# Two layer norms ahead of a state-space stage, moved from VectorE to ScalarE and GpSimd, with the norm's affine folded into the projections

## The chip, the cores and the metric

One Trainium2 chip, one core. The metric is the device time of the kernel in microseconds (us); lower is better. TensorE (PE), VectorE (DVE), ScalarE (ACT), GpSimd (POOL) and SyncE (SP, which here only issues transfers) each run an instruction stream of their own, in order, and wait for each other on semaphores. "In order" is the thing to keep in mind: an instruction whose operands are ready still waits for everything ahead of it on its engine.

## The reference, cut to what matters

Two blocks follow each other on x of shape (4, 2048, 256), fp32. Only the head of the first block matters here:

```python
h  = layernorm(x) * (1 + ca) + sa                       # first norm, modulated by row vectors
mu = mean(h); var = mean((h - mu) ** 2)
xn = (h - mu) / sqrt(var + 1e-5) * norm_w + norm_b      # second norm, of the state-space stage
z    = xn @ W_in
gate = silu(xn @ W_gate)
dt   = clip(softplus(z @ W_dt + b_dt), 0.001, 1.0)
Bp, Cp = z @ W_B, z @ W_C
# 16 states, scanned over time:  state = exp(dt * A) * state + (dt * Bp * z);  y_t = sum_s state_s * Cp_s
y = scan(...) * gate
x = x + ga * (h + y @ W_out)
# then: a second norm and a gelu FFN (block 0); attention-like scan, RWKV and two expert FFNs (block 1)
```

## The kernel before, in words

**Tiles.** The 8192 tokens are cut into 16 chunks of 512. Channels by tokens or tokens by channels, a chunk is 128 partitions wide. Weights and the activations that feed them are split into a high and a low part, and such a product is three matmuls (`split3`, line 1548).

**Streams.** Every engine's order is written out ahead by `weave`. The backbone is the state-space stage of chunk i: 23 empty marks, 68 units (16 states by 4 blocks of 128 channels, and 4 more to drain), then a tail that gates y, turns it, multiplies by W_out and adds. Three side streams are merged into the backbone by the table `PACE`, which gives each piece of a stream the backbone step ahead of which it is issued: `n_stream` (the front of the stage: both norms, xn, the projections, dt), `f_stream` (block 0's FFN, one chunk behind) and `x_stream` (block 1, two chunks behind). A step number below zero lies in the steps of the chunk before. One engine's pieces of one stream keep their order.

**A unit.** For unit u (state s, channel block d) ACT computes exp(dt * A) into one of two PSUM banks (A0, A1; line 1105), POOL computes its input z * B into one of four buffers `bu` (line 960), DVE runs the scan (line 1329), PE turns the result to tokens (four transposes, line 1543) into bank H0 or H1, and DVE adds it, times C, into `acc` (the read-out, line 1279). ACT may fill a bank once the scan two units back has read it; POOL may fill a buffer once the scan four units back is done.

**The norms ahead of the stage.** On DVE, for the four token tiles of a chunk: `stats` (bn_stats line 1251, bn_aggr line 1255), POOL takes the power -0.5 (line 947), DVE centres and scales (lines 1263, 1268, with the modulation rows `cA0`, `sA0`), `stats` again, POOL's power and bias (lines 951, 953), and ACT applies it (`n_norm`, line 1040). PE turns n; ACT evicts it with norm_w as scale and norm_b as bias into `xnf` (line 1052) and copies the high part `xnh` (line 1057); DVE subtracts for `xnl` (line 1301). `bu` lies over `xnh` and `xnl`, and the projections use banks A0 and A1, so they can't start before the last scan of the chunk before. In the table the DVE pieces `mean0`, `norm0`, `mean1` stand at -4, -4, -3: behind the last unit, ahead of the tail's `out`.

**The tail.** DVE multiplies `acc` by the gate in token layout (`gated`, line 1339), PE turns it (`y`), ACT copies it out (line 1118), PE multiplies by W_out (line 1564), DVE adds.

**PE's order from the last units on**: h2T of block 1 between units 63 and 64, the four last turns of the scan, the four kq products, y, kvT, btT, out0, qsT, out1, then xn0, xn1, ao0, ao1, then bc, dt, gate, ct, z (the front's 78 matmuls of 512 columns and a few small ones), then block 1's xlT and the FFN's c0 to c7.

Of the kernel before, what the change touches and what calls it, by code (L numbers as in the profile page):

```python
# [145 lines left out]
def since(eng, sig, chunk, k=0):  # L146

    if sig.at(chunk, k) > 0:
# [10 lines left out]
    },  # L159
    "pool": {  # L160
        "rstd0": -157, "rstd1": -108, "gx": 3, "u0": 20, "u1": 21, "u2": 27, "u3": 27, "xg": 95, "rstd_a": 103,
        "x_prob": 147, "rstd_e": 187, "x_bias": 190, "rstd_h": 209, "rstd_i": 210, "rstd_j": 214, "rstd_m": 241,
        "x5": 286,
    },
    "act": {
# [1646 lines left out]
```

## Time and profile before

| | |
|---|---|
| median of 3 runs | 3481.04 us (3476.44 to 3485.96) |
| the profiled execution's own time | 3472.46 us |
| its span, first to last instruction | 3470.7 us |
| busy, share of the span: PE | 2944.9 us (85%) |
| DVE | 2869.9 us (83%) |
| ACT | 2037.2 us (59%) |
| POOL | 1748.8 us (50%) |
| mean granted TensorE clock | 0.925 |
| first scans of chunks 5, 6 and 7 start at | 1066.3, 1261.2, 1457.5 us |
| last scans of chunks 5, 6 and 7 end at | 1202.6, 1398.0, 1596.8 us |

So a chunk takes some 196 us: some 137 us from its first scan to its last, and some 59 us from there to the first scan of the next. The shares say that PE and DVE are close to each other and that neither is full; they do not say where which of them is waited for. In the rows below a timeline row is: start, duration, engine, line, operation, tiles out<-in, count, and in brackets how long the engine sat idle ahead of it and who ended that. A group row is: line, engine, operation, tiles, shapes, count, then busy us in total, mean ns of one, and idle us ahead of it.

### The profile page before, as it was taken

To read this page: it belongs to the slowest core of one execution; us is meant where nothing else is said; L and a number is where in the kernel's file an instruction comes from. 1 tells how busy PE (TensorE), PEld (TensorE's weight loads), DVE (VectorE), ACT (ScalarE), POOL (GpSimd) and SP (SyncE) were. 2 spreads that over 40 slices of the span, in tenths; PEclk is the share of its full clock that TensorE was granted. 3 is DMA by queue.
4 is the path that set the end of the run, shared out by engine and by line. 5 is a ranking of instruction groups with operands and counts; after the bars stand their busy time and mean duration, and the time that the engine had idled before them with its cause. 6 is when DMAs were issued, how large, how long until landed. Compare 5 with 4: busy or idle time off the path is not lost. (4 is left out here: it accounts for less than half of the span.)

```text
span 3470.7 us, 45595 instructions
## 1 busy us (share of the span) xinstructions
PE 2944.9 (85%) x15032; PEld 2409.8 (69%) x15032; DVE 2869.9 (83%) x5084; ACT 2037.2 (59%) x3393; POOL 1748.8 (50%) x1389
## 2 busy tenths in 40 slices
PE   3567599898989899898989989898989899897957
PEld 1446478687777778687777778677777778676746
DVE  4596979898998989798998979899898979798231
ACT  0436476665757576665757576665757566574423
POOL 0555556464755656464755646464655646464010
PEclk7659599999999999999999999999999999998979
DMA  7112122231323223231312323131312323031302
GB/s 242 45 46 61 37 95 101 81 108 54 124 68 113 84 95 101 78 110 56 122 64 103 101 95 101 63 117 63 117 65 93 114 92 104 32 126 56 110 30 79
DMA packets 152906, 307.66 MB, mean 89 GB/s; under 512 B 18376, under 2 KB 97116, under 8 KB 135260
## 3 DMA queue, kind: packets, MB, share of 16 engines
q1 hardware_dynamic: 152128, 301.60, 26.1%
q8 instruction: 121, 1.98, 0.2%
q10 hardware_dynamic: 272, 1.57, 0.1%
q0 software_dynamic: 272, 1.57, 0.1%
q14 instruction: 113, 0.93, 0.1%
HBM read 287.35 MB, written 17.36 MB: 88 GB/s over the span
## 5 line engine op out<-in xcount | busy, mean ns | idle before, releaser
L960 POOL TENSOR_TENSOR bu<-z,bb 128x512 f32<-128x512 f32 x1024 | 1299.9, 1288 | 494.6 <-DVE hs L1329 303.7
L1105 ACT ACTIVATE ps_A<-dt,a_neg 128x512 f32<-128x512 f32 x1024 | 701.5, 687 | 606.6 <-DVE hs L1329 603.3
L1329 DVE TENSOR_TENSOR_SCAN hs<-ps_A,state,bu 128x512 f32<-128x512 f32 x768 | 974.4, 1273 | 37.1 <-ACT ps_A L1105 19.4
L1543 PE MATMUL ps_H<-ident,hs 128*128 128x128 f32 x4096 | 652.0, 298 | 222.4 <-DVE acc L1279 125.4
L1543 PEld LDWEIGHTS ps_H<-ident,hs 128*128 128x128 f32 x4096 | 520.7, 152 | 360.0 <-DVE acc L1279 164.1
L1662 PE MATMUL ps_B<-ws_out,hid 128*128 128x256 f32 x3072 | 722.1, 381 | 18.2 <-ACT hid L1243 10.5
L1279 DVE SCALAR_TENSOR_TENSOR acc<-ps_H,ctok,acc 128x512 f32<-128x512 f32 x960 | 697.5, 728 | 21.9 <-PE ps_H L1543 19.0
L1662 PEld LDWEIGHTS ps_B<-ws_out,hid 128*128 128x128 f32 x3072 | 568.7, 190 | 101.7 <-ACT hid L1243 15.5
L1548 PE MATMUL ps_B<-fh,ws_in 128*128 128x512 f32 x1536 | 572.1, 418 | 8.3 <-ACT cb L1215 4.2
L1548 PEld LDWEIGHTS ps_B<-fh,ws_in 128*128 128x128 f32 x1536 | 290.0, 189 | 69.0 <-ACT cb L1215 10.4
L1329 DVE TENSOR_TENSOR_SCAN hs<-ps_A,bu 128x512 f32<-128x512 f32 x256 | 309.7, 1211 | 27.0 <-ACT ps_A L1105 19.5
L1548 PE MATMUL ps_B<-fl,ws_in 128*128 128x512 f32 x768 | 301.0, 392 | 0.0
L1241 ACT ACTIVATE hid<-ps_B 128x512 f32<-128x512 f32 x256 | 150.7, 589 | 151.2 <-PE ps_B L1548 150.8
L1548 PE MATMUL ps_B<-f1h,ws_in 128*128 128x512 f32 x512 | 189.4, 433 | 53.9 <-DVE lg L1361 24.2
L990 POOL TENSOR_TENSOR z<-z,dt 128x512 f32<-128x512 f32 x64 | 88.4, 1382 | 164.3 <-ACT dt L1090 164.3
L1548 PEld LDWEIGHTS ps_B<-f1h,ws_in 128*128 128x128 f32 x512 | 104.8, 205 | 90.0 <-DVE lg L1361 25.7
L1243 ACT ACTIVATE hid<-hid 128x512 f32<-128x512 f32 x256 | 161.7, 632 | 8.2
L1548 PEld LDWEIGHTS ps_B<-fl,ws_in 128*128 128x128 f32 x768 | 146.1, 190 | 20.5
L1519 DVE SCALAR_TENSOR_TENSOR hA<-ps_B,coef,hA 128x256 f32<-128x256 f32 x192 | 79.6, 476 | 94.9 <-PE ps_B L1662 93.3
L1396 DVE TENSOR_TENSOR fl<-ff,fh 128x512 fp32r<-128x512 f32 x64 | 47.6, 784 | 132.2 <-ACT fh L1177 132.2
L951 POOL TENSOR_TENSOR rs_x<-rs_x,mhalf 128x4 f32<-128x4 f32 x48 | 52.9, 1103 | 190.1 <-DVE rs_x L1259 190.1
L947 POOL TENSOR_TENSOR rs_s<-rs_s,mhalf 128x4 f32<-128x4 f32 x16 | 18.9, 1184 | 206.3 <-DVE rs_s L1259 206.3
(245 smaller groups left out, 4566.0 us busy)
## 6 DMA issues: line engine op xcount, KB each, us to landing
ws_in<-w_split SPq DMA_DIRECT2D x128, 1024.0 KB, 5.0
bb<-b_rows SPq DMA_DIRECT2D x256, 256.0 KB, 4.0
ws_out<-in_L_ffn_V_rwkv SPq DMA_DIRECT2D x64, 512.0 KB, 5.6
ws_out<-in_L_ffn_W SPq DMA_DIRECT2D x32, 512.0 KB, 5.8
w_split<-ws_in SPq DMA_DIRECT2D x8, 1024.0 KB, 5.2
xb<-in_L_attn_x SPq DMA_DIRECT2D x16, 512.0 KB, 7.3
n<-in_L_attn_x SPq DMA_DIRECT2D x16, 512.0 KB, 3.9
out<-xb SPq DMA_DIRECT2D x16, 512.0 KB, 2.8
```

The costliest lines, as they stand in the source:

```text
L951: pool.tensor_tensor(rs[:, :], rs[:, :], mhalf[:, :], ALU.pow).then_inc(own_sig.sem, 1)
L960: pool.tensor_tensor(bu[:, u % 4, :], z[:, d, :], bb[:, s % 2, :], ALU.mult)\
L990: pool.tensor_tensor(z[:, k, :], z[:, k, :], dt[:, k, :], ALU.mult).then_inc(s_u.sem, 1)
L1105: act.activation(b.t[:, :], dt[:, d, :], ACT.Exp, scale=a_neg[:, d, s:s + 1])\
L1241: act.activation(hid[:, k, :], b.t[:, :], ACT.Relu).then_inc(b.free, 1)
L1243: act.activation(hid[:, k, :], hid[:, k, :], ACT.Square).then_inc(x_sq.sem, 1)
L1279: dve.scalar_tensor_tensor(out=acc[:, t, :], in0=b.t[:, :], scalar=ctok[:, t, s:s + 1], in1=acc[:, t, :], op0=ALU.mult, op1=ALU.add).then_ ...
L1329: dve.tensor_tensor_scan(hs[:, s % 2, d, :], b.t[:, :], bu[:, k % 4, :], state[:, s, d:d + 1] if i % CPB else 0.0, ALU.mult, ALU.add)\
L1519: ins = dve.scalar_tensor_tensor(out=hA[:, t, :], in0=b.t[:, t % 2 * C:(t % 2 + 1) * C], scalar=coef[:, t, e:e + 1], in1=hA[:, t, :], op0= ...
L1543: return pe.transpose(dst, src, ident[:, :])
L1548: last = pe.matmul(dst, a, b, start=n == 0, stop=n == len(prods) - 1)
L1662: last = pe.matmul(b.t[:, t % 2 * C:(t % 2 + 1) * C], hid[:, k, t * P:(t + 1) * P], wt[:, k % HB, :], start=k == 0 and t % 2 == 0, stop=k ...
```

## The change

- DVE's pieces `mean0`, `norm0`, `mean1` and the two powers of `n_stream` on POOL are replaced. ACT sums a token tile with an activation that has an accumulator output (`sum0`), POOL makes the negative mean, ACT sums the squares of x minus mean (`sq0`, Square with bias), POOL makes rstd and the bias (`rstd0`), ACT normalizes in place (`norm0`), POOL multiplies by `cA0` and adds `sA0` (`h0`: two operations on 128x1024), and the same for the second norm (`sum1`, `sq1`, `norm1`).
- norm_w is multiplied into the high and low parts of W_in, W_gate, the product W_in W_dt and the narrow weights; norm_b goes through the weights into bias columns (`in_col`, `bdt_col`). This is done once, in the setup. ACT's eviction into `xnf` goes; `xnh` and `xnl` are made from PSUM.
- The gate is computed channels by tokens, like z, and is multiplied on DVE where ACT copied the turned y out of PSUM. The step `gated` goes: a chunk has 98 steps in place of 99.
- The table `PACE` is new as a whole.

The core of the diff, POOL's part first, then ACT's, then DVE's:

```diff
                 def n_stream(i):
+                    for n in range(2):
+                        yield f"mean{n}"
+                        pool.wait_ge(s_sum.sem, s_sum.at(i, n + 1))
+                        pool.tensor_scalar(nm_s[:, :], sum_s[:, :], -1.0 / C, None, ALU.mult).then_inc(s_nm.sem, 1)
+                        yield f"rstd{n}"
+                        pool.wait_ge(s_sq.sem, s_sq.at(i, n + 1))
+                        own.step(pool.tensor_scalar(rs_s[:, :], sq_s[:, :], 1.0 / C, EPS, ALU.mult, ALU.add))
+                        own.step(pool.tensor_tensor(rs_s[:, :], rs_s[:, :], mhalf[:, :], ALU.pow))
+                        pool.tensor_tensor(nb_s[:, :], nm_s[:, :], rs_s[:, :], ALU.mult).then_inc(s_rs.sem, 1)
+                        if n == 0:
+                            yield "h0"
+                            pool.wait_ge(s_norm.sem, s_norm.at(i, 1))
+                            own.step(pool.tensor_tensor(x[:, :, :], x[:, :, :], per_tile(m_row("cA0")), ALU.mult))
+                            pool.tensor_tensor(x[:, :, :], x[:, :, :], per_tile(m_row("sA0")), ALU.add)\
+                                .then_inc(s_h0.sem, 1)
...
                 def n_stream(i):
+                    for n, (ready, at) in enumerate(((s_xin, 16), (s_h0, 1))):
+                        yield f"sum{n}"
+                        for t in range(NT):
+                            ins = act.activation(n0[:, t, :], x[:, t, :], ACT.Identity, accum_out=sum_s[:, t:t + 1])
+                        yield f"sq{n}"
+                        for t in range(NT):
+                            ins = act.activation(n0[:, t, :], x[:, t, :], ACT.Square, bias=nm_s[:, t:t + 1],
+                                                 accum_out=sq_s[:, t:t + 1])
+                        yield f"norm{n}"
+                        apply((x, n0)[n], x, rs_s, nb_s, (s_norm, s_n)[n])
                     for c in range(KC):
-                        act.activation(xnf[:, c, :], b.t[:, :], ACT.Identity, scale=cols[:, c:c + 1],
-                                       bias=cols[:, 2 + c:3 + c]).then_inc(b.free, 1)
+                        act.activation(xnh[:, c, :], b.t[:, :], ACT.Copy).then_inc(s_xnh.sem, 1)
...
-                    if name == "gated":
-                            ins = dve.tensor_tensor(acc[:, t, :], acc[:, t, :], gate[:, t, :], ALU.mult)
+                    if name == "y":
+                        used(dve, i, f"gt{k}")
+                        b = take(dve, i, f"y{k}")
+                        dve.tensor_tensor(yT[:, k, :], b.t[:, :], gate[:, k, :], ALU.mult).then_inc(b.free, 1)
```

Where the new table puts things, in steps of the new count (units 0 to 63 are steps 23 to 86, so of the chunk before they are -75 to -12): ACT `sum0` -50, `sq0` -40, `norm0` -29, `sum1` -21, `sq1` -14, `norm1` -8; POOL `mean0` -49, `rstd0` -34, `h0` -24, `mean1` -17, `rstd1` 10 (behind block 1's `x_bias` and `x5`), `xg` 38 (was 95). On PE, kq0 to kq3 are interleaved with the last four turns instead of following them, xn0 stands ahead of y2 and xn1 ahead of ao0; ao0, ao1 still stand ahead of bc, and the order bc, dt, gate, ct, z is kept. On ACT `lexp` and c0's eviction come ahead of the first exp of the chunk (they came behind it), and both gelu pieces are one behind the other.

## Rows read from the trace of the kernel before

**Rows 1.** Windows: length, busy us (count) of PE, PEld, DVE, ACT, POOL, clock, DMA share, GB/s.

```profile
1261.00:1388.00 127.00, 121.16 (x654) 101.44 (x652) 123.70 (x165) 87.03 (x145) 83.48 (x67) 1.00 0.33 112
1388.00:1398.00 10.00, 3.94 (x16) 3.14 (x16) 9.92 (x20) 4.04 (x7) 6.20 (x5) 0.61 0.15 52
1398.00:1427.00 29.00, 25.78 (x145) 21.81 (x146) 24.41 (x71) 11.67 (x21) 8.39 (x7) 0.96 0.06 19
1427.00:1447.00 20.00, 19.61 (x91) 15.64 (x90) 15.82 (x54) 14.01 (x25) 3.85 (x4) 1.00 0.43 127
1447.00:1457.00 10.00, 6.44 (x32) 4.37 (x30) 3.48 (x8) 9.94 (x17) 6.24 (x5) 0.90 0.00 0
```

**Rows 2.** PE's timeline between two chunks.

```profile
1393.21 1.12 PE L1543 MATMUL ps_H<-ident,hs 128*128 128x128 f32 x4 [5.79 <-DVE acc L1279]
...
1402.02 3.24 PE L1705 MATMUL ps_B<-w_kq,ff 128*128 128x304 f32 x12
1406.41 0.66 PE L1543 MATMUL ps_H<-ident,acc 128*128 128x128 f32 x4 [1.15 <-DVE acc L1339]
...
1411.56 1.06 PE L1543 MATMUL ps_B<-ident,bx 128*128 128x128 f32 x8 [0.85 <-ACT ca L1202]
...
1426.72 0.48 PE L1548 MATMUL ps_A<-xnh,w_nar_h 128*128 128x512 f32 x1
```

**Rows 3.** DVE's groups of instructions, shapes apart, whole run.

```profile
L1251 DVE BATCH_NORM_STATS2 st_s<-xb 128x6 f32<-128x256 f32 x128 | 44.8, 412 | 7.3 <-DMA xb<-in_L_attn_x 7.2
L1339 DVE TENSOR_TENSOR acc<-acc,gate 128x512 f32<-128x512 f32 x64 | 39.9, 686 | 0.4 <-issue 0.3
L1268 DVE SCALAR_TENSOR_TENSOR xb<-xb,rs_s,mod_s 128x256 f32<-128x256 f32 x64 | 26.8, 481 | 0.6
L1263 DVE SCALAR_TENSOR_TENSOR xb<-xb,mv_s,mod_s 128x256 f32<-128x256 f32 x64 | 26.6, 476 | 0.0
L1255 DVE BATCH_NORM_AGGREGATE mv_s<-st_s 128x2 f32<-128x6 f32 x128 | 11.9, 156 | 1.4
```

**Rows 4.** ACT's groups of instructions, shapes apart, whole run.

```profile
L1105 ACT ACTIVATE ps_A<-dt,a_neg 128x512 f32<-128x512 f32 x1024 | 701.5, 687 | 606.6 <-DVE hs L1329 603.3
L1099 ACT ACTIVATE state<-hs 128x4 f32<-128x4 f32 x256 | 49.9, 195 | 6.7 <-DVE hs L1329 6.7
L1118 ACT ACTIVATE yT<-ps_H 128x512 f32<-128x512 f32 x64 | 38.1, 595 | 125.4 <-PE ps_H L1543 125.4
L1040 ACT ACTIVATE n<-xb,nb_s,rs_s 128x256 f32<-128x256 f32 x64 | 33.2, 590 | 139.0 <-POOL nb_s L953 139.0
L1052 ACT ACTIVATE xnf<-ps_A,cols 128x512 f32<-128x512 f32 x32 | 23.3, 773 | 22.0 <-PE ps_A L1543 21.9
```

**Rows 5.** POOL's groups of instructions, shapes apart, whole run.

```profile
L960 POOL TENSOR_TENSOR bu<-z,bb 128x512 f32<-128x512 f32 x1024 | 1299.9, 1288 | 494.6 <-DVE hs L1329 303.7 <-DMA bb<-b_rows 182.4 <-POOL z L990 3.6
L985 POOL TENSOR_TENSOR xb<-xb,mod_s 128x1024 f32<-128x1024 f32 x16 | 37.8, 2364 | 37.2 <-ACT n L1040 37.2
L951 POOL TENSOR_TENSOR rs_s<-rs_s,mhalf 128x4 f32<-128x4 f32 x16 | 16.1, 1008 | 85.0 <-DVE rs_s L1259 85.0
```

**Rows 6.** DVE's timeline: two scans that follow each other.

```profile
1348.53 1.27 DVE L1329 TENSOR_TENSOR_SCAN hs<-ps_A,state,bu 128x512 f32<-128x512 f32 x1
...
1350.36 1.27 DVE L1329 TENSOR_TENSOR_SCAN hs<-ps_A,state,bu 128x512 f32<-128x512 f32 x1
```

**Rows 7.** The first chunk: DVE's and ACT's timelines.

```profile
85.61 1.40 DVE L1251 BATCH_NORM_STATS2 st_s<-xb 128x6 f32<-128x256 f32 x4 [7.24 <-DMA xb<-in_L_attn_x]
...
94.46 2.07 ACT L1040 ACTIVATE n<-xb,nb_s,rs_s 128x256 f32<-128x256 f32 x4 [60.33 <-POOL nb_s L953]
```

**Rows 8.** PE's timeline between chunks 0 and 1.

```profile
253.79 7.14 PE L1564 MATMUL ps_H<-w_out,yT 128*128 128x256 f32 x32 [0.88 <-ACT yT L1118]
260.77 1.04 PE L1543 MATMUL ps_A<-ident,n 128*128 128x128 f32 x8
265.18 0.50 PE L1548 MATMUL ps_A<-xnh,w_nar_h 128*128 128x512 f32 x1 [3.37 <-DVE xnl L1301]
```

More of the change, by code:

```diff
@@ L53 @@
 UNIT_STEPS = [("unit", u) for u in range(DS * DB + DB)]
-TAIL_STEPS = [("gated", 0)] + [("y", k) for k in range(DB)] + [("out", 0), ("out", 1), ("x1", 0)]
+TAIL_STEPS = [("y", k) for k in range(DB)] + [("out", 0), ("out", 1), ("x1", 0)]
 S_STEPS = MARKS + UNIT_STEPS + TAIL_STEPS
@@ L635, in _ @@
                 pe.wait_ge(u_ctc, 1)
+                pe.wait_ge(u_nw, 32)
+                for m in range(2 * DB):
+                    for c in range(KC):
+                        last = pe.matmul(psum["A0"][:, C + m:C + m + 1], staged(0)[:, c, m * P:(m + 1) * P],
+                                         cols[:, 2 + c:3 + c], start=c == 0, stop=c == KC - 1)
+                last.then_inc(u_bias, 1)
                 mod_rows(0)
@@ L650, in _ @@
                 last.then_inc(u_prod, 1)
+                for m in range(DB):
+                    for d in range(DB):
+                        last = pe.matmul(psum["A0"][:, C + 2 * DB + m:C + 2 * DB + m + 1],
+                                         staged(1)[:, d, m * P:(m + 1) * P], in_col[:, d:d + 1],
+                                         start=d == 0, stop=d == DB - 1)
+                for d in range(DB):
+                    last = pe.matmul(psum["A0"][0:2 * DS, C + 3 * DB:C + 3 * DB + 1], w_bc_in[:, d, :],
+                                     in_col[:, d:d + 1], start=d == 0, stop=d == DB - 1)
+                last.then_inc(u_bias, 1)
                 for k in range(KC):
@@ L1051, in n_stream @@
                         b = take(act, i, f"xn{c}")
-                        act.activation(xnf[:, c, :], b.t[:, :], ACT.Identity, scale=cols[:, c:c + 1],
-                                       bias=cols[:, 2 + c:3 + c]).then_inc(b.free, 1)
-                    for c in range(KC):
-                        yield f"xnh{c}"
-                        used(act, i, f"xn{c}")
-                        act.activation(xnh[:, c, :], xnf[:, c, :], ACT.Copy).then_inc(s_xnh.sem, 1)
+                        act.activation(xnh[:, c, :], b.t[:, :], ACT.Copy).then_inc(s_xnh.sem, 1)
                     yield "bc"
@@ L1064, in n_stream @@
                         act.wait_ge(s_state.sem, s_state.at(i - 1, DS - 1))
-                    act.activation(bcs[:, :], b.t[0:2 * DS, :], ACT.Copy).then_inc(b.free, 1)
+                    act.activation(bcs[:, :], b.t[0:2 * DS, :], ACT.Identity, bias=in_col[0:2 * DS, 2 * DB:2 * DB + 1])\
+                       .then_inc(b.free, 1)
                     for k in range(DB):
@@ L1070, in n_stream @@
                         act.activation(dt[:, k, :], b.t[:, :], ACT.Exp, bias=bdt_col[:, k:k + 1]).then_inc(b.free, 1)
-                    for k in range(NT):
+                    for k in range(DB):
                         yield f"gate{k}"
-                        since(act, s_yg, i)
+                        if i:
+                            used(act, i - 1, f"y{k}")
                         b = take(act, i, f"gt{k}")
-                        act.activation(gate[:, k, :], b.t[:, :], ACT.Silu).then_inc(b.free, 1)
+                        act.activation(gate[:, k, :], b.t[:, :], ACT.Silu, bias=in_col[:, DB + k:DB + k + 1])\
+                           .then_inc(b.free, 1)
                     yield "ct"
@@ L1085, in n_stream @@
                         b = take(act, i, f"z{k}")
-                        act.activation(z[:, k, :], b.t[:, :], ACT.Copy).then_inc(b.free, 1)
+                        act.activation(z[:, k, :], b.t[:, :], ACT.Identity, bias=in_col[:, k:k + 1])\
+                           .then_inc(b.free, 1)
                     for k in range(DB):
@@ L1282, in n_stream @@
                 def n_stream(i):
[L1283 to L1297 removed]
                     for c in range(KC):
                         yield f"xnl{c}"
+                        b = take(dve, i, f"xn{c}")
                         dve.wait_ge(s_xnh.sem, s_xnh.at(i, c + 1))
[L1301 to L1302 removed]
+                        dve.tensor_tensor(xnl[:, c, :], b.t[:, :], xnh[:, c, :].bitcast(F32), ALU.subtract)\
+                           .then_inc(b.free, 1)
                     for k in range(DB):
@@ L1581, in n_stream @@
                     yield "bc"
-                    pe.wait_ge(s_xnl.sem, s_xnl.at(i, KC))
+                    for c in range(KC):
+                        used(pe, i, f"xn{c}")
                     from_xn(i, "bc", narrow["bc"], 0)
@@ L1586, in n_stream @@
                         from_xn(i, f"dt{k}", w_dt, k * P)
[L1587 removed]
+                    for k in range(DB):
                         yield f"gate{k}"
[L1589 to L1593 removed]
+                        from_xn(i, f"gt{k}", w_in, DI + k * P)
                     yield "ct"
@@ L1616, in step @@
                     if name == "y":
-                        pe.wait_ge(s_yg.sem, s_yg.at(i, 1))
+                        for use in (DS * NT - 2, DS * NT - 1):
+                            used(pe, i, f"hT{use}")
                         b = fill(pe, i, f"y{k}")
```

131 lines of the change are left out of this document (63 added, 68 removed), and 62 rows, old and new, of the table PACE.

## The prediction

> **What bounds the kernel now.** The page first: PE 85%, DVE 83%, and no single wait that would explain the rest. The chain that ended last covers only the last chunk's block 1, so it doesn't help for a change at the head of every chunk. I therefore cut one chunk of the steady state (chunk 6) into windows, with the first and last scan as bounds [rows 1]. The reader is to see a bound that changes hands three times. From the first scan to 1388, DVE works 123.70 of 127 us: DVE bounds, and PE, at 121.16, is hardly less full. From 1388 to 1398 DVE is full and PE, with 3.94 of 10, waits for it. From the last scan (1398) to the first projection matmul of the next chunk PE works 25.78 of 29 us, and from there to the end of the z projections 19.61 of 20: PE bounds. In the last 10 us ACT is full (9.94) with softplus, evictions and the first exp. Over the whole chunk DVE and PE have 177 us of work each in 196.
>
> So the place of the removed work decides. The two norms on DVE stand between the last scan and the W_out products, where DVE has some slack (24.41 of 29) and PE doesn't.
>
> **What the change takes from DVE.** Per chunk: 8 bn_stats, 8 aggregates, 4 centres and 4 finishes, in total (44.8 + 11.9 + 26.6 + 26.8) / 16 = 6.9 us [rows 3]. The `gated` product (39.9 / 16 = 2.5 us) is not saved: the same 4 products of 128x512 come back at `y`, with PSUM as one source. If DVE's time were worth its face value this would be 6.9 x 16 = 110 us. It isn't, because PE's queue between the chunks holds the same matmuls as before and the front (bc to z) still stands behind out0, out1, ao0 and ao1 there.
>
> **What PE gets back.** Only its idle time in the 29 us can go: 29 - 25.78 = 3.2 us [rows 1]. Of this, 1.15 is y waiting for `gated`, 0.85 is a turn waiting for ACT's kvT eviction, which stands behind ACT's y copies [rows 2], and the rest is small waits of the same kind. With `gated` gone and no y copies on ACT all but some 0.7 us should go: -2.5. Then h2T and kq0 are pulled ahead of turns that wait for the last scans. PE idles there (3.94 of 10 us busy, one wait of 5.79 us) [rows 1, 2], and a kq product is 3.24 / 3 = 1.1 us [rows 2]; block 1's h2T must wait for its own norm first, so I count 0.9 of it: -0.9. The front then starts 3.4 us earlier. What used to be late next, DVE's second norm, isn't: it is done in the chunk before.
>
> Behind the front the last 10 us belong to ACT. There c0's eviction is now ahead of the first exp; the nearest row is a PSUM eviction of the same shape, 595 ns [rows 4]: +0.6. `lexp` ahead of it costs nothing, since DVE waited for it anyway before its first scan. Per boundary between chunks: -2.8.
>
> **What ACT and POOL must now hide.** In the 127 us ACT has 40 us free and POOL 43 [rows 1], so the sum isn't the question, but the order is: each piece is a block ahead of an exp or of a `bu`. Two scans start 1.83 us apart [rows 6]. ACT may start the exp of unit u+2 when scan u ends, it takes 0.69 [rows 4], and it is needed 2 x 1.83 - 1.27 = 2.4 us after that end. A block starts when the exp before is done, 1.83 - 0.69 = 1.1 before it. `norm` is four activations, 2.07 us [rows 7]: it ends at +1.0, the exp at 1.7, with 0.7 to spare. What the accumulator output adds is in no row. Lower bound: nothing, Square and Identity as fast as this. Upper bound: a further short instruction each, like the 128x4 activation of 195 ns [rows 4], so 2.07 + 0.8 = 2.9 us, and the exp at 2.5: late by 0.1. But in this stretch block 1's experts need pairs of evictions of 0.6 us each, and a block beside such a pair (1.2 more) is late by 0.5 to 1.3, either for the scan or for a down product on PE, which is as full as DVE there. Five blocks a chunk lie in the scans (`sum0`, `sq0`, `norm0`, `sum1`, `sq1`), the last beside DVE's own long insert. I take 1.0 us a chunk, between 0 and 4 (three blocks at 1.3).
>
> POOL: `h0` is 2 x 2.364 = 4.7 us ahead of one `bu` [rows 5]. POOL may be up to four units ahead: buffer u is needed 4 x 1.83 - 1.27 = 6.1 us after scan u-4 ends, and `h0` can start when the `bu` before is done, 1.83 - 1.29 = 0.5 before it: 4.7 - 0.5 + 1.3 = 5.5 us. It fits by 0.6. `xg` (2.4 us) fits too, and the small operations on 128x4 are about 1 us each at most, the power 1.008 [rows 5]. I cost POOL at 0; without that cover it would be at most 5.5 - 6.1 plus one more power, 0.4 a chunk. ACT's `norm1` waits for POOL's `rstd1` behind `x_bias` and `x5`, two more operations of 2.4 us: some 4 us after the last scan, while PE reaches xn0 some 8 us after it.
>
> Can POOL's new work hold DVE up directly? The trace shows DVE 123.70 and POOL 83.48 busy in one window of 127 us [rows 1], so at least 80 us of POOL's two-operand products run beside DVE, the scans and read-outs still 1.83 us apart: no. The Trainium skill (SBUF — State Buffer, section "Who interferes with whom") has DVE contend with GpSimd's reads only where DVE reads two operands from SBUF; by that rule the scans and read-outs, with one operand in PSUM, stay free, and the trace agrees. By its shorter advice (Perfetto Trace Analysis, "Optimizing Scalar/DVE Operations"), that moving work between DVE and GpSimd might not help because of the shared port, `h0` would be paid in full; that is a rival below.
>
> **The start.** In the first chunk nothing covers the chain. Before, from the landing of x (85.61) to the end of n (96.53) it took 10.9 us [rows 7]. Now: four sums and two norms of 2.07 = 12.4, with 0 to 0.8 more on each of the sums; `h0` 4.7; two powers at 1.0; six small POOL operations at 0.2 (a guess near ACT's 195 ns) 1.2; some ten handovers at 0.15: about 22 to 25, so +11 to +14. `xnf` is skipped: the pair of evictions at 773 ns in front of the copies goes [rows 4]: -1.5. The setup gets some 40 one-column matmuls and a few small DVE operations: +1 (between 0 and 4; the loads of weights are waited for there anyway). Together +12.
>
> **Chunk 0 to 1.** Without block 1 PE is idle there: y waits for `gated`, and after xn PE waits 3.37 us for `xnf`, `xnh`, `xnl` [rows 8]. Now xn1 follows out1 and needs one ACT copy and one DVE subtraction, but DVE's stats for the FFN stand between. From 265.18 to about 261: -4.
>
> **The end.** After the last chunk the same 3.4 us of PE idling go: -3.
>
> **Sum.** 14 boundaries x (-2.8 + 1.0) = -25; +12 - 4 - 3: -20 us. Against the profiled execution (3472.46) that is 3452; it lies 0.25% under the median of the runs, so for the median 3481.04 - 20 = 3461. Faster by 0.6%; a difference of under 0.3% (10 us) could not be told from none.
>
> **Rivals.**
> - *The blocks on ACT eat the gain.* At 2.8 us a chunk of lateness all boundaries are worth nothing and the start alone remains: 3481 + 5 = 3486. At 4 us a chunk, the upper bound, 3481 + 14 x 1.2 + 5 = 3503. For it: PE and DVE are both over 95% full in the scans, so any lateness shows at once. Against: ACT is idle for a third of that window. It ends slower by more than 0.3% from 3.2 us a chunk on. 0.30, of which 0.16 slower.
> - *DVE is the bound after all*, because the new order lets PE work move into the scans: up to 6.9 us a boundary, 14 x -6.9 + 5 = -92, 3390. Against: PE has only 6 us free in those 127, and ao and out stay in front of bc. 0.06; half way (3425) another 0.06.
> - *`h0` holds DVE up* for its 4.7 us: 14 x (4.7 - 1.8) + 5 = +46, 3527. Against: the overlap just shown. 0.03.
> - *xn0 comes too early on PE*: it now stands ahead of y2, and if `norm1` is later than PE, everything behind it waits, out0 included. From 4 us lateness on it costs more than is gained; at 6 us 14 x 2 + 5 = +33, 3510. 0.05.
>
> The forecast (3461, its own range 3443 to 3478) has 0.50. Faster than 0.3%: 0.61, within it 0.19, slower 0.20. The range for 8 in 10 is 3425 to 3503.
>
> **What the profile after would show.** The four norm lines gone from DVE, DVE's busy time down by some 110 us and the span by far less. PE's first projection matmul some 25.6 us after the last scan in place of 28.7, and PE's idle time there under 1 us. Gaps between scans some 1 us a chunk longer in total, released by ACT. In the first chunk xn some 12 us later. Wrong would be: the 137 us from first to last scan longer by over 3 us, an activation with accumulator above 0.72 us, PE waiting for `n` ahead of y2, or PE's order turning out to leave idle time elsewhere.

## The result, and the profile after

The changed kernel takes 3403.35 us (median of 4 runs, 3403.0 to 3407.58), the kernel before, run beside it, 3483.5 us: a ratio of 0.9768, 95% interval 0.9743 to 0.9793. Faster by 2.3%, where 0.6% was forecast, and outside the range. The profiled spans are 3401.4 and 3470.7 us, 69.3 apart; all that follows is read within these two (the profiled execution of before lies some 10 us under the median of its runs, hence 69 and not 80).

Read from VectorE's timeline, as first and last scan of every chunk (us; the means within and between chunks are over chunks 2 to 14):

| stretch | before | after | difference | forecast |
|---|---|---|---|---|
| start to the first scan of chunk 0 | 129.5 | 141.7 | +12.2 | +12 |
| chunk 0 to chunk 1 | 52.4 | 49.2 | -3.2 | -4 |
| first to last scan of a chunk | 137.3 | 135.4 | **-1.9** | **+1.0** |
| last scan to first projection matmul | 28.3 | 24.4 | -3.9 | -3.4 |
| projections, bc to z | 20.3 | 20.5 | +0.2 | 0 |
| from there to the next first scan | 10.5 | 10.8 | +0.3 | +0.6 |
| last scan of all to the end | 300.7 | 299.1 | -1.6 | -3 |

Added up over the chunks, the stretches between first and last scans give 28 us of the 69 (forecast: 14 us lost), the 14 boundaries 48 (forecast: 39 gained); the start takes 12 back, chunk 0 to 1 and the end give 5.

The windows of chunk 6 after the change, cut like those of before [rows 1]: length, then busy us (count) of PE, PEld, DVE, ACT, POOL, clock, DMA share, GB/s.

```profile
1245.00:1371.00 126.00, 120.08 (x652) 100.68 (x650) 124.28 (x166) 93.30 (x178) 92.89 (x75) 1.00 0.30 97
1371.00:1381.00 10.00, 5.22 (x19) 4.08 (x20) 9.22 (x19) 5.00 (x10) 7.19 (x7) 0.67 0.16 54
1381.00:1405.00 24.00, 23.08 (x141) 19.91 (x140) 17.37 (x40) 7.25 (x14) 3.57 (x3) 1.00 0.07 23
1405.00:1426.00 21.00, 20.52 (x98) 16.49 (x97) 15.64 (x54) 14.81 (x25) 3.84 (x4) 1.00 0.63 222
1426.00:1436.50 10.50, 6.84 (x34) 4.96 (x33) 4.06 (x9) 10.44 (x18) 7.25 (x6) 1.00 0.00 1
```

Third row: between the last scan and the first projection PE now works 23.08 of 24 us. The waits for `gated`, for the y copies and for `nn` are gone, as forecast; of the 0.85 us for kvT's eviction 0.52 are left. DVE has 17.37 us there instead of 24.41: the 7 us left DVE and only 3.9 came back, since PE bounds. ACT and POOL carry 6 and 9 us more in the first row; the stretch from first to last scan hasn't become longer for it, but a little shorter.

PE's timeline between the chunks (start, duration, what, and in brackets the idle time before it and what ended it):

```profile
1376.88 1.97 PE L1591 MATMUL ps_B<-ident,nE 128*128 128x128 f32 x8 [0.61 <-ACT nE L1088]
1379.72 1.99 PE L1751 MATMUL ps_B<-w_kq,ff 128*128 128x304 f32 x4
...
1390.33 0.63 PE L1591 MATMUL ps_B<-ident,bx 128*128 128x128 f32 x4 [0.52 <-ACT ca L1264]
...
1405.24 0.48 PE L1596 MATMUL ps_A<-xnh,w_nar_h 128*128 128x512 f32 x1
```

kq0 stands at 1379.72, one us ahead of the last scan's end (1380.7), and nothing waits for `gated`; the first projection is at 1405.24.

The ACT groups with the accumulator, and those that got a bias column:

```profile
L1106 ACT ACTIVATE n<-xb,nm_s 128x256 f32<-128x256 f32 x128 | 63.1, 494 | 0.7 <-POOL nm_s L1016 0.7
L1101 ACT ACTIVATE n<-xb 128x256 f32<-128x256 f32 x128 | 51.2, 401 | 49.2 <-DMA xb<-in_L_attn_x 44.3 <-POOL xb L1027 4.9
L1135 ACT ACTIVATE gate<-ps_A,in_col 128x512 f32<-128x512 f32 x64 | 42.4, 686 | 4.7 <-PE ps_A L1596 4.4
L1106 ACT ACTIVATION_READ_ACCUMULATOR n<-xb,nm_s 128x1 f32 x128 | 23.9, 187 | 0.0
```

The accumulator does bring an instruction of its own, of 187 ns, but it overlaps its activation; a sum and its read repeat every 0.40 us, a square every 0.49, so four of them are 1.6 and 2.0 us, no longer than an apply.

What DVE waited for in the scans, in the kernel before (group; busy us, mean ns; idle before, by releaser):

```profile
L1329 DVE TENSOR_TENSOR_SCAN hs<-ps_A,state,bu 128x512 f32<-128x512 f32 x768 | 974.4, 1273 | 37.1 <-ACT ps_A L1105 19.4 <-POOL bu L960 13.4 <-ACT state L1099 1.8
L1279 DVE SCALAR_TENSOR_TENSOR acc<-ps_H,ctok,acc 128x512 f32<-128x512 f32 x960 | 697.5, 728 | 21.9 <-PE ps_H L1543 19.0
L1386 DVE TENSOR_TENSOR xb<-xb,nn 128x1024 f32<-128x1024 f32 x16 | 22.0, 1378 | 0.0
```

and after:

```profile
L1377 DVE TENSOR_TENSOR_SCAN hs<-ps_A,state,bu 128x512 f32<-128x512 f32 x768 | 975.1, 1274 | 24.6 <-ACT ps_A L1167 13.5 <-POOL bu L997 6.8 <-issue 2.4
L1341 DVE SCALAR_TENSOR_TENSOR acc<-ps_H,ctok,acc 128x512 f32<-128x512 f32 x960 | 697.1, 727 | 4.4 <-PE ps_H L1591 3.0
L1434 DVE TENSOR_TENSOR xb<-xb,nn 128x1024 f32<-128x1024 f32 x16 | 20.5, 1279 | 0.0
```

The scans and read-outs take the same time, beside busier engines; what went is waiting: 37.1 to 24.6 us and 21.9 to 4.4. By unit, over chunks 2 to 14, before's waits for exp at units 2 and 3 (12 us), for `bu` at unit 8 (12) and for exp behind the gelus at unit 19 (5) are gone or small, none of them near a norm. New are 9.4 us at unit 62 (exp behind `e_norm`), 5.8 at unit 30 (`bu` behind `x_prob`).

The waits at units 2 and 3 have a cause of their own, TensorE's clock. In the kernel before, the granted clock over the first four units was 0.70 to 0.72 in four of these 13 chunks (2, 7, 10 and 14) and 0.96 to 1.00 in nine. The four take 138.9 us from first to last scan, the nine 136.6. After the change it is 1.00 in all 13. The first 7 us of chunks 6 and 7 before:

```profile
1261.10:1268.10 7.00, 7.00 (x34) 5.73 (x33) 6.63 (x7) 5.93 (x11) 6.84 (x7) 1.00 0.48 160
1457.40:1464.40 7.00, 7.00 (x23) 5.48 (x23) 4.62 (x5) 3.99 (x8) 6.84 (x7) 0.69 0.18 34
```

PE is busy throughout in both, but at 0.69 it gets through 23 matmuls instead of 34. So in chunk 7 ACT's eviction of the feed-forward waits for PE, the exp stands behind it, and the scan waits for the exp:

```profile
1459.88 0.69 ACT L1149 ACTIVATE hid<-ps_B,b_col 128x512 f32<-128x512 f32 x1 [1.83 <-PE ps_B L1548]
1461.28 1.28 DVE L1329 TENSOR_TENSOR_SCAN hs<-ps_A,state,bu 128x512 f32<-128x512 f32 x1 [1.32 <-ACT ps_A L1105]
```

Four chunks at 2.3 us are 0.7 us of the 1.9 a chunk.

### The profile page after: what moved, and what is told of

It is laid out like the page before. It is cut to its first block and busy times, and to the rows that moved or that the text cites. A ratio compares the mean times of both kernels' runs of the same rounds, so it can differ in the third digit from the quotient of the medians.

```text
span 3401.4 us, 45813 instructions
## 1 busy us (share of the span) xinstructions
PE 2930.5 (86%) x15104; PEld 2407.5 (71%) x15104; DVE 2755.0 (81%) x4626; ACT 2096.5 (62%) x3843; POOL 1837.9 (54%) x1501
## 5 line engine op out<-in xcount | busy, mean ns | idle before, releaser
L1377 DVE TENSOR_TENSOR_SCAN hs<-ps_A,state,bu 128x512 f32<-128x512 f32 x768 | 975.1, 1274 | 24.6 <-ACT ps_A L1167 13.5
L1708 PE MATMUL ps_B<-ws_out,hid 128*128 128x256 f32 x3072 | 730.5, 381 | 2.8 <-ACT hid L1219 2.6
L1708 PEld LDWEIGHTS ps_B<-ws_out,hid 128*128 128x128 f32 x3072 | 558.1, 190 | 73.3 <-ACT hid L1305 3.9
L1596 PE MATMUL ps_B<-fh,ws_in 128*128 128x512 f32 x1536 | 585.8, 425 | 15.2 <-ACT rows_x L1184 10.8
L1596 PE MATMUL ps_B<-f1h,ws_in 128*128 128x512 f32 x512 | 180.6, 410 | 53.9 <-ACT rows_f L1184 20.6
L988 POOL TENSOR_TENSOR rs_f<-rs_f,mhalf 128x4 f32<-128x4 f32 x16 | 16.1, 1008 | 273.2 <-DVE rs_f L1321 273.2
L1596 PEld LDWEIGHTS ps_B<-f1h,ws_in 128*128 128x128 f32 x512 | 97.5, 190 | 83.4 <-issue 23.9
```

Source lines behind the costliest of these rows:

```text
L988: pool.tensor_tensor(rs[:, :], rs[:, :], mhalf[:, :], ALU.pow).then_inc(own_sig.sem, 1)
L1377: dve.tensor_tensor_scan(hs[:, s % 2, d, :], b.t[:, :], bu[:, k % 4, :], state[:, s, d:d + 1] if i % CPB else 0.0, ALU.mult, ALU.add)\
L1596: last = pe.matmul(dst, a, b, start=n == 0, stop=n == len(prods) - 1)
L1708: last = pe.matmul(b.t[:, t % 2 * C:(t % 2 + 1) * C], hid[:, k, t * P:(t + 1) * P], wt[:, k % HB, :], start=k == 0 and t % 2 == 0, stop=k ...
```

## The experiments

Theory A: the scans got shorter because the new merge moved pieces that have nothing to do with the norms; the blocks cost next to nothing. Theory B: the norms' move itself shortened them. Each run was timed beside the kernel before. In all kernels the measure within the profile is that of the table ("scans" is first to last scan of a chunk, "boundary" last scan to the next first scan). "Places" are the numbers of `PACE`, converted to the kernel's count of steps.

**e4: fewer sums on ACT.**

```diff
-                        for t in range(NT):
+                        for t in range(1 if i else NT):
                             ins = act.activation(n0[:, t, :], x[:, t, :], ACT.Identity, accum_out=sum_s[:, t:t + 1])
```

and the same for the squares: from chunk 1 on three of four token tiles keep stale statistics.

> The changed kernel, but from chunk 1 on ScalarE sums and squares only the first of four token tiles (the statistics of the other three are left stale): 3 x (401+187) + 3 x (494+187) = 3.8 us of ScalarE per norm, 7.6 us per chunk, are gone from the scans. If ScalarE's blocks cost nothing but the one late exp before unit 62 (0.7 us a chunk, theory A): 3392 to 3403, scans 134.7 to 135.4. If they cost what I had forecast or more (1.0 to 4 us a chunk, covered until now by other gains): 3340 to 3388, scans 131.5 to 134.4.

3406.8 us, ratio 0.978 (0.9761 to 0.9798). From first to last scan of chunk 6 (windows, the changed kernel first, then e4) ACT works 92.95 us instead of 97.94, and nothing follows:

```profile
1245.20:1380.70 135.50, 124.80 (x669) 104.47 (x668) 133.00 (x184) 97.94 (x186) 99.66 (x80) 0.98 0.29 94
```

```profile
1249.50:1385.30 135.80, 125.09 (x668) 104.40 (x668) 133.01 (x184) 92.95 (x162) 100.06 (x80) 0.98 0.29 94
```

Scans 135.5 us as well, and the total is 4 us above the first case's range, far from the second's. Of ScalarE's work 5 us are gone, not the 7.6 of the expectation, which had added the accumulator's reads, though they overlap. Sums and squares cost nothing where they stand.

**e1: norms back on VectorE; e2: the kernel before with the new places.** e1 in core; `...` stands for pieces left out:

```diff
 "pool": {
-"mean0": -49, "rstd0": -34, "h0": -24, "mean1": -17, "rstd1": 10
+"rstd0": -4, "rstd1": -3
 "act": {
-"sum0": -50, "sq0": -40, "norm0": -29, "sum1": -21, "sq1": -14, "norm1": -8, "xn0": -7
+"n_norm": -3, "xn0": -3
...
 "dve": {
+"mean0": -4, "norm0": -4, "mean1": -3
```

Behind the norms the front's own pieces stand at their old places in both, `xn0` to `gate2` on ACT and `xn0` to `dt1` on PE, and so do a_norm, h1T and h1h on ACT.

> The changed kernel with the two norms put back: statistics, modulation and second statistics on VectorE between the last unit and the projections, reciprocal roots on GpSimd, one apply on ScalarE, at the places of the kernel before; the folded weights, the gate by feature and the new merge of all other pieces stay. Measured so far from first to last scan of a chunk: 137.3 us before, 135.4 after; from last scan to the first projection 28.3 before, 24.4 after. Theory A (the shorter scans come from the new merge of pieces that have nothing to do with the norms; the norms' move gives the 3.4 us at the boundary and costs at most 0.7 us in the scans): scans stay at 134.7 to 135.4, the first projection comes 27.4 to 28 us after the last scan, first scan of chunk 0 back at about 130 us, total 3403 + 15 x 3.2 - 12 - up to 10 = 3430 to 3440. Theory B (the norms' move itself shortens the scans): scans back at 137.3, total 3460 to 3470.

> The kernel before, norms and gate as they were, with only the new places of all pieces that are not part of the norms (the feed-forward, the experts, the attention, the loads). Theory A (the scans are shorter through the new merge): scans 135.0 to 135.6 us instead of 137.3, boundary 59.1 less up to 0.9 for the earlier h2T and kq pieces, total 3483 - 16 x 1.9 - 14 x 0.5 = 3435 to 3455. Theory B (they are shorter through the norms' move): scans 137.0 to 137.5, total 3470 to 3485. Theory C (both are needed: the new merge only fits with the norms off VectorE): longer than before.

e1: 3575.44 us, ratio 1.0266 (1.0244 to 1.0288). e2: 3557.98 us, 1.0213 (1.0194 to 1.0231). The scans take 136.5 us in both: the new merge alone gives 0.8 of the 1.9. The other 1.1 comes only with the norms' pieces in the scans (how is shown under e12). But both are slower than before, by the boundary: 66.8 and 65.7 us instead of 59.1, theory C of e2; e1's expectation had neither. e1's PE shows why:

```profile
1663.21 6.72 PE L1597 MATMUL ps_H<-w_out,yT 128*128 128x256 f32 x16 [4.68 <-DVE yT L1373]
```

out0 waits 4.68 us for the fourth y eviction, which stands behind the norms in DVE's queue. Its 16 matmuls then take 6.72 us at a granted clock of 0.54; in e10 the same 16 take 3.69 at 1.00. So the wait is paid twice.

**e10: norms on VectorE behind the y evictions.** `mean0`, `norm0`, `mean1` and both `rstd` at -3.

> The changed kernel with both norms on VectorE as in e1, but placed behind the four y evictions instead of among them. In e1 PE waited 4.7 us for yT, because the fourth y eviction, which the change has given to VectorE, stood behind 5.2 us of norm work; first projection 34.5 us after the last scan. Theory: without that wait, but with the norms 1 us later, the first projection comes 30 to 33 us after the last scan and the total is 3500 to 3550; what is left over the changed kernel's 24.4 is the price of norms on VectorE under the new merge. Rival (the norms themselves are free there and e1's loss was the order alone): 25 to 27 us, total 3410 to 3440.

3563.81 us, ratio 1.0221 (1.0195 to 1.0246); first projection 33.7 us after the last scan, both a little above the theory's ranges. The wait moved on:

```profile
1651.88 3.69 PE L1597 MATMUL ps_H<-w_out,yT 128*128 128x256 f32 x16
...
1659.92 1.09 PE L1576 MATMUL ps_B<-ident,qx 128*128 128x128 f32 x4 [3.91 <-DVE cb L1453]
```

out0 is early, but now the attention's recurrence `cb` is behind the norms, PE waits 3.91 us for it, and xn behind that. In neither of the two places tried does the new merge leave room for 7 us of DVE at the boundary.

**e6: norms on ScalarE and GpSimd, but late.** All six ACT pieces at -8 to -5, POOL's at -10 to -8 (`rstd1` stays); the front's own pieces follow at their old places, as in e1.

> The changed kernel with the whole ScalarE and GpSimd norm chain behind the last bu and the last exp of the chunk instead of spread over 45 units of the scans. The chain by its own durations: two rounds of sums 4 x 0.49, squares 4 x 0.59 (with the accumulator reads), GpSimd 0.25, 0.2 + 1.03 + 0.2, apply 2.07, and h0 of 2 x 2.37 between, 2 x 7.9 + 4.7 = 20.5 us and the hops. Theory (the gain is that the norms are done during the scans, where both engines have room, not that another engine does them): first projection 32 to 42 us after the last scan instead of 24.4, scans 134.5 to 136, total 3403 + 15 x 8..17 = 3520 to 3660. Rival (ScalarE and GpSimd are free at the boundary too, PE's other work covers the chain): 24.4 to 28 us, total 3400 to 3460.

3589.23 us, ratio 1.029 (1.0272 to 1.0307); first projection 32.6 us after the last scan, scans 136.5.

```profile
1479.20 1.97 PE L1589 MATMUL ps_A<-ident,n 128*128 128x128 f32 x8 [4.09 <-ACT n L1086]
```

PE waits 4.09 us for `n`. Over the 7 us from there the granted clock is 0.55, and the projections too take 22.7 us instead of 20.5. This is e10's loss with the other engines. So the gain at the boundary comes from the norms being finished while VectorE scans; which engine frees that place is secondary. The chain is partly covered: 8.2 us later, not 17.

**e9 and e8: the places inside the scans.** e9 is the changed kernel with the pieces from lexp and c0 to e_stats, and from r0 to p7, at their old places (79 places, moved by 1 to 26 steps); e8 the kernel before with these at the new ones. Of e9's edit:

```diff
 "pool": {
-"x_prob": 151
+"x_prob": 146
 "act": {
-"lexp": 121, "c0": 121, "c1": 122, "c6": 130, "c7": 134, "gelu0": 137, "gelu1": 137, "pb": 142
+"lexp": 122, "c0": 122, "c1": 123, "c6": 136, "c7": 136, "gelu0": 138, "gelu1": 140, "pb": 146
...
```

> The kernel before; only pieces of the feed-forward and the experts whose place lies well inside the scans (from lexp and c0 to x2 and e_stats, and from r0 to p7) take their new places; all that stands at the boundary, norms and gate stay as they were. Theory A (about 0.8 us of the 1.9 us by which the scans got shorter is this merge: VectorE's idle time in the scans fell from 3.7 to 2.4 us a chunk when the merge changed, with or without the norms): scans 136.3 to 136.8 us instead of 137.3, boundary 59.1 as before, total 3483 - 16 x 0.5..1.0 = 3467 to 3476. Theory B (the merge gives nothing by itself): 3480 to 3487.

> The changed kernel; the same pieces well inside the scans go back to their old places, norms, gate and boundary stay new. Theory A (half the scans' gain is this merge): scans 136.2 to 137.3 us instead of 135.4, boundary 55.7, total 3403 + 16 x 0.8..1.9 = 3416 to 3433. Theory B (the gain in the scans comes with the norms on ScalarE and GpSimd, which put GpSimd's multiplications out of the way of VectorE's long ones): 3400 to 3408. The two xb<-xb+nn and fl<-ff-fh of VectorE tell it: 1.2 us and 0.68 us where no GpSimd multiplication runs beside them, 1.9 and 1.3 where one does.

e9: 3490.98 us, ratio 1.0008 (0.9995 to 1.0022). Scans 140.6 us, boundary 56.0. This is more than either theory had: the norms' move with the old places gains its 3 us at the boundary and loses 3.3 in the scans. e8: 3515.87 us, ratio 1.008 (1.0065 to 1.0095). Its scans take 136.8 instead of 137.7 us, compared over the ten chunks other than 4, 8 and 12, in which PE came 10 to 11 us late at unit 38, a loss that neither original has. There PE waits for a load of expert weights:

```profile
961.47 3.75 PE L1661 MATMUL ps_B<-ws_out,hid 128*128 128x256 f32 x8 [9.65 <-DMA ws_out<-in_L_ffn_V_rwkv]
```

SP issued that load at 955.99, right behind the load of `mod_f` (955.63), which kept its old place and comes once in four chunks: old and new places clash. From the end of the projections to the first scan e8 takes 1.2 us longer, and its end 9. Only the ten chunks speak on the question.

In e9 one loss can be followed. Its POOL, then its ACT:

```profile
1517.62 2.39 POOL L1054 TENSOR_TENSOR xb<-xb,pb 128x1024 f32<-128x1024 f32 x1 [7.56 <-ACT pb L1222]
1519.96 1.29 POOL L995 TENSOR_TENSOR bu<-z,bb 128x512 f32<-128x512 f32 x1
```

```profile
1514.24 0.40 ACT L1099 ACTIVATE n<-xb 128x256 f32<-128x256 f32 x1
...
1515.85 1.70 ACT L1222 ACTIVATE pb<-mod_f,prob 128x256 f32<-128x256 f32 x4
```

```profile
1521.28 1.28 DVE L1375 TENSOR_TENSOR_SCAN hs<-ps_A,state,bu 128x512 f32<-128x512 f32 x1 [0.99 <-POOL bu L995]
```

`sum0` stands on ACT right ahead of `pb`, for 1.6 us. POOL's `x_prob` waits 7.56 us for `pb`, `bu` stands behind `x_prob`, and the scan waits 0.99 us, in every chunk. In the changed kernel `pb` runs 7 us ahead of `sum0` (1280.81 and 1288.14). A block on ACT that makes others late is what I had forecast, though as a late exp and not by way of `pb`, `x_prob` and `bu`; the change had taken it out.

Most of the rest goes with the clock. In five of the 13 chunks the granted clock over the first four units is 1.00, and the scans take 138.5 us; in eight it is 0.75 to 0.79, and they take 141.9. In the same eight a product of PE behind the late scan is slow too. Chunks 3 and 7:

```profile
738.14 3.69 PE L1610 MATMUL ps_B<-w,ca 128*128 128x256 f32 x16 [2.01 <-DVE ca L1533]
1524.50 5.38 PE L1610 MATMUL ps_B<-w,ca 128*128 128x256 f32 x16 [2.02 <-DVE ca L1533]
```

The granted clock over the 5.5 us from there is 1.00 in the first and 0.69 in the second, and in the second the read-out of unit 27 waits 1.5 us for PE. The wait of 2.0 us ahead is the same in both. In the kernel before it is 1.3 to 1.4, and the product takes 3.69 us in all 13 chunks. Compared at a full clock, e9's 138.5 us are 1.9 over before's 136.6. Of these 1.0 is the `bu` at unit 25 and 0.7 the exp behind `e_norm` at unit 62. The latter is not a norm's: e1 and e2, without the norms' blocks, have it as well (9.3 us over the 13 chunks). It is `e_norm`'s own new place, which e11 takes back.

**e14 and e13: one group of places each.** e14: only the first feed-forward's pieces old (24 places, POOL as changed). e13: only `x_prob` 151 to 146.

> The changed kernel; only the pieces of the first feed-forward (lexp, c0 to c7, both gelus, pb, d0 to d7 and the two loads of its second weights) go back to their old places, one to six units later; GpSimd and the second expert stay new. Theory (these places carry most of the 5.2 us that e9 lost: late exps at units 2 and 3 and behind the first gelu, PE late for acc at units 15, 25 to 28): scans 138 to 140.5 us instead of 135.4, total 3440 to 3480. Rival (the 5.2 us are spread, or come from GpSimd): scans 135.5 to 137, total 3405 to 3425.

> The changed kernel with GpSimd's x_prob alone at its old place, five units earlier. Theory (behind x_prob and the mean and reciprocal-root steps of the norms bu comes late, 1.0 us at unit 25 in e9): the 0.45 us stall at unit 30 goes and one of 0.5 to 1.0 us comes at unit 25, scans 135.4 to 136.1, total 3403 to 3413. Rival: no difference by place, 3400 to 3406.

e14: 3496.3 us, ratio 1.0036 (1.0023 to 1.0049), scans 141.9 us. This is more than the theory's 138 to 140.5, and the main reason is another. ACT at unit 18:

```profile
1309.91 1.28 ACT L1217 ACT_TABLE_LOAD   x1
1311.21 1.91 ACT L1217 ACTIVATE hid<-hid 128x2048 f32<-128x2048 f32 x1
1313.03 2.06 ACT L1086 ACTIVATE nn<-hA,nb_x,rs_x 128x256 f32<-128x256 f32 x4
1315.10 1.28 ACT L1165 ACT_TABLE_LOAD   x1
```

The old gelu1 falls right ahead of the new `m_norm`: 6.5 us between two exps, and DVE waits 3.8 us a chunk. It is a clash of an old place with a new one; no norm of the change is in it. The clock has its share here as well: the scans take 140.6 us in five chunks and 142.6 in eight with 0.75 to 0.79 over the first four units. So e14 can't share out e9's 5.2 us, and neither can e9 be read as the price of the norms alone. e13: 3411.31 us, ratio 0.9783 (0.9768 to 0.9797), scans 135.8: the wait at unit 30 went, no wait came at unit 25, and it is slower all the same, since DVE's subtractions `fl` now meet `bu` (928 ns on average instead of 795).

**e12: does GpSimd slow VectorE?** `x2` on VectorE from 159 to 160.

> The changed kernel with one VectorE piece, the addition xb<-xb+nn over 1024 columns, one unit later. It runs now while GpSimd does the 4-column steps of a reciprocal root, and takes 1.21 us; where a GpSimd multiplication bu<-z*bb ran beside it (e1, e2, some chunks of before) it took 1.88. Theory (the two share a path to SBUF): one unit later it meets bu and takes 1.8 to 1.9 us, scans 136.0 to 136.1 instead of 135.4, total 3403 + 15 x 0.65 = 3413. Rival (the times differ for another reason): it takes 1.21 us, total 3400 to 3406.

3421.15 us, ratio 0.9812 (0.9792 to 0.9832), scans 136.4 us. The group:

```profile
L1432 DVE TENSOR_TENSOR xb<-xb,nn 128x1024 f32<-128x1024 f32 x16 | 31.8, 1986 | 0.0
L1375 DVE TENSOR_TENSOR_SCAN hs<-ps_A,state,bu 128x512 f32<-128x512 f32 x768 | 973.4, 1272 | 24.0 <-ACT ps_A L1165 11.6 <-POOL bu L995 8.1 <-issue 2.6
```

1279 ns became 1986; the scans themselves stay at 1272. The theory holds, with a somewhat higher price. This is the other part of theory B: in e1 and e2, without the norms' small POOL steps in its queue, `bu` runs beside `x2` (1840 and 1870 ns) and more of the subtractions `fl` (928 ns on average instead of 795), by the means 0.6 + 0.5 = 1.1 us a chunk, and e1's scans are 1.1 us longer than the changed kernel's. e6 has the norms on the new engines, but not in the scans, and goes with e1. Per chunk, over chunks 2 to 14 (us):

| | first to last scan | VectorE idle in it | `x2` and the two `fl` in it |
|---|---|---|---|
| before | 137.3 | 3.4 | 2.7 |
| e2 | 136.5 | 1.9 | 3.9 |
| e1 | 136.5 | 2.0 | 3.9 |
| e6 | 136.5 | 2.0 | 3.8 |
| changed | 135.4 | 2.1 | 2.6 |

The second column is also the price of the blocks in the new order: with them VectorE idles 0.1 us more than without (e1).

**e5: the kq pieces.** PE's h2T 184 to 185, kq 185, 186, 188 to 187, 189, 189, and DVE's the same.

> The changed kernel with PE's h2T and kq pieces and VectorE's kq pieces at their old places, one to three units later. As forecast (0.9 us of the boundary's gain is these pieces leaving PE's queue after the last scan): the first projection matmul comes 25.3 us after the last scan instead of 24.4, total 3403 + 14 x 0.9 = 3416. Rival (they are in VectorE's or PE's idle time anyway): 3400 to 3407. Third (they were better late, for the scans): below 3400.

3437.07 us, ratio 0.9856 (0.9841 to 0.987). The first projection comes 26.6 us after the last scan, +2.2 instead of +0.9, but it isn't one value: 25.0 in four of the 13 boundaries, 26.4 in one and 27.2 to 27.7 in eight. One of the first and one of the last kind (chunks 2 and 6), the first 10 us behind the last scan:

```profile
620.90:630.90 10.00, 9.43 (x60) 7.60 (x60) 8.42 (x18) 5.05 (x10) 2.57 (x2) 1.00 0.01 2
1393.00:1403.00 10.00, 9.90 (x44) 8.23 (x45) 6.57 (x15) 2.52 (x6) 2.53 (x2) 0.72 0.01 2
```

At a clock of 1.00 PE gets through 60 matmuls, at 0.72 through 44. Ahead of both PE had worked 3.94 of 10 us. In the second PE spent about half of the 10 us at the lower of its two levels (1.2 and 2.4 GHz). So at a full clock the moved work is 0.6 us (0.9 forecast), and the rest of the 2.2 is the clock. In the changed kernel, with 5.22 of the 10 us ahead busy, the clock of the first 10 us behind the last scan of chunk 6 was 0.98.

**e11: e_norm behind the late exp.** ACT's `e_norm` 183 to 184.

> The changed kernel with ScalarE's e_norm one unit later, as it stood before the change. VectorE's idle time of 0.72 us a chunk at unit 62 is a late exp behind e_norm (four 0.52 us applies). Theory: the exp comes in time, scans 134.7 to 135.0 us instead of 135.4, total 3391 to 3398. Rival (e_norm is then late for PE's h2T, and the kq pieces slip behind the last scan as in e5): boundary 0.5 to 2.2 us longer, total 3403 to 3430.

3414.87 us, ratio 0.9795 (0.9775 to 0.9815). Both came: scans 134.6 us (-0.8), boundary 56.75 (+1.1), with the first projection that much later behind the last scan. Chunk 0 to 1 and the end are longer too (+2.4, +5.5).

**e7: the first chunk's norms on VectorE.**

```diff
+                    if i == 0:
...
+                        stats(own, x, st_f, mv_f, rs_s, s_mv)
...
+                        centre(own, x, x, mv_f, m_row("cA0"))
...
+                        finish(x, x, rs_s, lambda t: m_row("sA0"), s_h0)
...
+                        stats(own, x, st_f, mv_f, rs_s, s_mv, nm_s)
```

> The changed kernel with the norms of the first chunk alone on VectorE and GpSimd as before. The first scan came 12.2 us later after the change. If that is the ScalarE and GpSimd chain at the start: first scan at about 131 us, total 3391 to 3393. If it is the set-up (the folding of norm_w and norm_b, more in the first loads): first scan still at 139 to 142 us and total 3400 to 3404.

3396.46 us, ratio 0.9742 (0.9725 to 0.9758): the lowest median of all. First scan at 131.7 us, span 3391.3, 10.1 under the changed kernel's; by the timed runs 7 us, with intervals that overlap. Everything after chunk 0 is the same to 0.1 us.

**e3: all feed-forward and expert pieces old**, those of the boundary too. 14 places on SP, 6 on POOL, 30 on ACT, 21 on DVE, 44 on PE.

> The changed kernel with the norms' new place and engines, and the pieces of the feed-forward and the experts within the scans at their old places (those at the boundary as in the changed kernel). Theory A: scans 137 to 138.5 us (the old stalls back, with the ScalarE and GpSimd blocks on top), boundary unchanged at 55.7, total 3403 + 16 x 1.9 = 3433, up to 3450. Theory B: scans 135.4, total 3400 to 3410.

3723.93 us, ratio 1.0688 (1.067 to 1.0707). Scans 138.5, but the projections took 36.1 instead of 20.5 us: PE waits 13.51 us for ACT's `bcs`, which stands behind `a_norm`, whose reciprocal root is on POOL behind `rstd_h` and `rstd_i`, which wait for DVE. A mixture of two orders, outside both theories and no evidence on the question; e9 replaced it.

## Why the prediction was wrong

**The step that failed** is the term for the blocks on ACT and POOL in the scans, +1.0 us a chunk between 0 and 4. Measured from first to last scan: -1.9 (42 us of the 49 by which the sum was off). It priced the blocks in the order of the kernel before, and it let the new places of more than 100 other pieces count for nothing there, without a reason.

What the runs show in its place, per chunk:
- The new order alone gives 0.8 (e2): VectorE's waits fall by 1.4 us, and its SBUF-only operations meet `bu` more often and take 1.2 more; the remainder is spread over many small differences. Half of the 1.4 is waits that the kernel before had in four chunks with a TensorE clock of about 0.7 at their start. The prediction had the clock in no term.
- The norms' pieces in the scans give another 1.1 (against e1 and e6). The blocks themselves cost 0.1 of waiting, and GpSimd's small steps keep `bu` off `x2` and `fl`. This was luck; nothing in the prediction looked for it.
- With the old places inside the scans (e9) the forecast mechanism is real: at a full clock the late `bu` behind `sum0` costs 1.0 us a chunk. That this is the figure of the forecast is chance; there it was spread over five blocks and came by late exps. The wait at unit 27 comes on top, on average 0.9. That it follows from the same late scan, by way of the clock, is likely but was not tested. The whole change is then worth nothing (ratio 1.0008), which is my first rival in its result.

Open stays why the clock falls at some of the equal boundaries. In the kernel before PE works 6.8 to 8.0 us of the 10.8 ahead of a first scan, the four low chunks 7.0 to 7.4. In eight chunks the clock is 0.84 to 0.90 over these 10.8 us already, and in four of the eight it stays low into the units. With the old places around the feed-forward's c pieces 4, 8 and 8 of 13 chunks are low (before, e9, e14), but none in e3; with the new ones none in eleven kernels, but 2 in e8.

**Point by point.**
- The bound was read rightly: 6.9 us left DVE per boundary and 3.9 came back, since PE bounds there (23.08 of 24 us busy). The rival with DVE as the bound (6.9 us back, so 21.4 us to the first projection) fell: PE's own work there is 23 us. That the measured 3403 lies between this rival's 3390 and its half way, 3425, is chance.
- -3.4 for the front, -3.9 measured. The moved h2T and kq are 0.6, not 0.9, at a full clock; without them the clock was low behind nine of 13 last scans, and on average they are worth 2.2 (e5). PE's clock was in no term: 0.96 before [rows 1], 1.00 after in this window.
- Not seen: under the new merge the norms at the boundary cost 8 to 10 us, on either pair of engines (e1, e10, e6). I had valued their going by the old order, at part of 2.5 us. Part of the 8 to 10 is again the clock (0.89, 0.94 and 0.92 over the stretch, 0.99 in the changed kernel).
- ACT's c0 ahead of the first exp: +0.3 against +0.6.
- Accumulator bounds 0 to 195 ns: at the low end, 0.40 and 0.49 us a tile against 0.52 for an apply.
- POOL at 0: `h0` caused no wait. `bu` behind `x_prob` costs 0.45 us a chunk at unit 30, but in e1 and e2 as well; it is `x_prob`'s new place and no norm's. The rival that `h0` holds DVE up fell: the scans stay at 1274 ns.
- First chunk +12, measured +12.2, by two errors that cancel: the chain from the first sum to the end of n took 20.8 us (89.26 to 110.03), not 22 to 25, and x landed 3.65 us later (85.61 to 89.26), not 1.
- Chunk 0 to 1 and the end: -3.2 and -1.6 against -4 and -3.
- xn0 too early on PE: no; it waits for nothing at 1387.44. (By its own sum this rival's time is 3481 + 33 = 3514, not 3510.)

## What to carry to other kernels

A change that comes with a new order is two changes, and the order can be the larger: price each moved piece's neighbours, who stands behind it in the queue and who is late then, above all for the waits that the profile of before already lists. Look at them chunk by chunk: a mean can hide that some of equal chunks ran at a lower clock, and that a kernel pays for a short wait of PE in slow matmuls behind it. Free the engine that bounds by finishing work in a stretch where others have room; which engine takes it matters less. And test one half of a merged order with suspicion: old and new places clash (e3, e8, e14), so a slow hybrid is no proof.

## What the runs showed of the hardware

- DVE's additions and subtractions with both inputs and output in SBUF slow down beside a GpSimd product that had started ahead of them: 1024 columns 1.21 us alone, up to 2.22 beside `bu` (e12), 512 columns 0.68 and up to 1.34. Where DVE had started first, it kept its time and GpSimd paid: in the changed kernel `fl` at 1435.85 takes 0.68 us and the `bu` that starts at 1435.98 1.70 instead of 1.28. Over six kernels (before, changed, e1, e2, e12, e13) DVE was slowed in 180 of the 182 cases in which `bu` had started first, and in none of the 70 in which DVE had. Operations with one input in PSUM (scan 1274, read-out 727 ns) don't slow down. The Trainium skill (SBUF — State Buffer, "Who interferes with whom") says that a DVE instruction with two SBUF inputs contends with GpSimd's reads and one with at most one, outside the two-port modes, doesn't, and the trace agrees; I had used it only for the scans and read-outs, and not for the three SBUF-only operations in their midst. GpSimd's operations on 128x4 don't slow DVE: in the changed kernel `x2` stands beside three of them, at 1.21 us.
- An activation of 128x256 from SBUF takes 401 ns bare (Identity), 494 with a bias column (Square), 590 with scale and bias columns; one of 128x512 from PSUM takes 595 ns as a copy and 686 with a bias column.
- The same boundary of the same program, with 3.94 of 10 us busy ahead of it, ran its first 10 us at a granted clock of 1.00 or 0.72, and took 25.0 or 27.6 us to the first projection (e5). Inside the scans, behind the same wait of 2.0 us, 16 matmuls took 3.69 us in five chunks and 5.38 at 0.69 in eight (e9).
